# Cross-attention and mixture of experts on one core: the attention slots rewritten as one cyclic schedule

## The chip, the cores and the metric

The kernel runs on one core of one Trainium2 chip. The metric is the device time of one execution, in microseconds (us). A core has five engines that work side by side, each in the order in which its instructions are written: TensorE (PE, with its weight loads shown apart as PEld), VectorE (DVE), ScalarE (ACT), GpSimd (POOL) and SyncE (SP), which here only issues transfers. They wait for one another on semaphores. TensorE writes its results to eight PSUM banks of 512 fp32 columns; DVE and ACT read them from there.

## What is computed

64 sequences `x` of 128 tokens by 128 features attend to 64 contexts of 120 tokens (16 heads of 8 features), and the result goes through a mixture of 8 experts of which each token uses its best two:

```python
x = x + attention(layernorm(x), ctx, ctx)          # softmax over the 120 keys, 16 heads, then Wo
# mixture of experts on h = layernorm(x)
probs = softmax(h @ Wr.T)                          # 8 experts
topv, topi = top_k(probs, 2)
x = x + sum_over_the_two(topv * (gelu(h @ W1[e] + b1[e]) @ W2[e] + b2[e]))
```

## The kernel before, in words

**Chunks and slots.** The 64 sequences go in 32 chunks of two. The attention part is a software pipeline of slots n = -2 to 33, all written out: in slot n the kernel finishes the attention of chunk n and prepares chunk n+1 (its queries) and chunk n+2 (its keys), while chunks n-1 and n-2 get their residual, second layer norm and routing. After the slots come 39 expert tiles of 512 token rows and a last stage that adds the expert results to `xres` and writes the output.

**What one slot does.** The names are those of the tiles in the profile.

- Projections (L1223 to L1225): four groups of six 128x256 matmuls, two for queries and two for keys, each into one bank. ACT takes a part of the bank (`part`, L1056, in `halve`) and DVE subtracts it from the bank into `qs` or `ks` (L711, in `unsplit`).
- SP copies `qs` to `qb` and `ks` to `kb`, four DMAs each (L351, L359). The copies lay the heads out in blocks, so that one matmul serves four heads.
- Scores by query (L1263, `by_query`): eight matmuls of 480 columns; DVE takes the maximum of each over the keys (`mx`, L717, in `best`).
- The maxima are turned on TensorE (L1386), negated and split in an upper and a lower part by DVE (`negm`, L881 and L883), and SP copies them into two rows of `qb` by two DMAs (L384).
- Scores by key (L1273, `by_key`): eight matmuls of 512 columns from `ks` and `qb`, which now hold the maxima too. ACT takes the exponential of each (`pt`, L1065).
- Weighing (L1285, `weigh`): for each exponential, four matmuls with 32-column weights, each at its own column position of the array; a trace shows eight instructions for them. They fill the bank `heads`.
- ACT copies the heads out (`ots`, L1146), TensorE turns them (L1244), DVE divides (`rden` L672, `on` L676), TensorE turns again (L1249), ACT copies (`onT`, L1154), TensorE multiplies by Wo (L1253), DVE adds to `xres` (L686).
- Layer norm: DVE statistics (L827 to L836), a power on GpSimd (`root`, L544), then four small DVE steps (L727 `yy`, L730 `vyy`, L733 `y`, L735 `shift`), ACT applies it.
- Routing: logits (L1394), top two, position of each row in its expert's list, and four scatters by GpSimd (L538). In slots 3 to 18 GpSimd also splits one block of expert weights in upper and lower parts (L602, L604, `wsp`).

**Order.** The order on each engine is the order of the calls in its `slot`. On TensorE each `weigh` is followed by one `by_key`, and `by_query` comes in pairs after them:

```python
for t in range(8):
    weigh(s, t, n)
    if t < 6:
        by_key(s, t + 2, n)
    ...
    if exists(n, 1) and 2 <= t < 6:
        by_query(c, 2 * t - 4, n)
        by_query(c, 2 * t - 3, n)
```

Banks have fixed uses: three (`wide`) for projections and scores by query, two (`scores`) for scores by key, one for `heads`, two (`small`) for everything else. A query goes from its projection through `qs`, the scores by query and the maxima within one slot; the scores by key of that chunk open the next slot.

**The end of attention.** In slot 31 TensorE counts the rows per expert so far (`early`, L1356). On that count SP writes eight 528 KB blocks of empty rows behind the experts' lists (L391, `xd<-zrows`); the last two chunks are scattered over them only afterwards, and the expert tiles read the lists (`rows<-xd`).

## Time and profile before

| | |
|---|---|
| median of 3 runs | 918.71 us (908.99 to 921.09) |
| the profiled execution | 902.89 us, of which the span from first to last instruction is 901.1 us |
| mean granted TensorE clock | 0.932 of full speed |
| attention, first to last slot's scores by key | from 40.5 us to 549 us |
| expert tiles | from 570 us to about 840 us |
| last stage | to 901 us |

Times in rows are microseconds from the span's start. "Busy" is the time in which an engine executes; "idle before" is what stood in front of an instruction on its engine, with what ended that wait.

### The profile page before, as it was taken

What the parts mean: (1) busy time and instruction counts of PE and PEld (TensorE: products, weight loads), DVE (VectorE), ACT (ScalarE), POOL (GpSimd) and SP (SyncE); (2) the same over time, 40 slices, a digit from 0 to 9 for tenths busy, and PEclk for the clock granted to TensorE, in tenths of its full rate; (3) what the DMA queues carried; (4) which work ended last, traced back from release to release, by engine and by line L of the source; (5) the groups of instructions that cost most, each with busy time, mean ns of one, the idle gap of its engine ahead of it and who ended that gap; (6) DMA issues with size and microseconds to landing.
All of it is one profiled execution on the core that took longest, in us unless ns stands there. A gap on an engine that the chain in (4) does not pass through costs nothing.

```text
span 901.1 us, 19693 instructions
## 1 busy us (share of the span) xinstructions
PE 762.4 (85%) x5606; PEld 548.7 (61%) x5606; DVE 670.5 (74%) x2135; ACT 613.6 (68%) x1131; POOL 477.2 (53%) x715
## 2 busy tenths in 40 slices
PE   3699999999999999999999976799889899998700
PEld 3456666566566665666666653588677687777500
DVE  4578889899988898888889873577465666656536
ACT  4677777777777677787777753688585777867500
POOL 4212656656556565554645434447656466675720
PEclk8699999999999999999999995699999899999955
DMA  5333454554545544343433315787666677776059
GB/s 176 97 80 77 116 153 126 135 149 132 154 126 140 150 125 126 106 102 87 99 95 83 88 43 215 234 278 250 212 192 194 197 230 236 228 229 194 18 203 356
DMA packets 117887, 140.33 MB, mean 156 GB/s; under 512 B 20431, under 2 KB 76134, under 8 KB 117799
## 3 DMA queue, kind: packets, MB, share of 16 engines
q1 hardware_dynamic: 105079, 115.72, 45.8%
q0 software_dynamic: 9088, 17.07, 5.5%
q10 hardware_dynamic: 3632, 6.49, 1.9%
q8 instruction: 41, 0.67, 0.3%
q14 instruction: 47, 0.39, 0.1%
HBM read 73.40 MB, written 36.08 MB: 121 GB/s over the span
## 4 chain that ended last, share of the span: by engine, by line
PE 61%; DVE 14%; issue 9%; DMA 5%; SPq 4%; ACT 4%; POOL 2%; another core or an unknown queue 1%; POOLq 0%; DVEq 0%; ACTq 0%
PE bank L1285 8%; PE bank L1273 8%; DVE mx L717 6%; PE bank L1263 5%; PE bank L1442 3%; PE bank L1440 3%; PE bank L1223 3%; PE bank L1441 3%; PE bank L1428 3%; PE bank L1425 3%; PE bank L1426 3%; DMA qb<-yd 3%; PE bank L1244 3%; PE bank L1225 3%; PE bank L1224 3%
## 5 line engine op out<-in xcount | busy, mean ns | idle before, releaser
L642 POOL DMA_INDIRECT yd<-vs,idt x156 | 161.3, 1034 | 105.8 <-DVE vs L991 55.1
L1065 ACT ACTIVATE pt<-bank,mpair 120x512 f32<-120x512 f32 x256 | 171.7, 687 | 48.3 <-PE bank L1273 44.1
L538 POOL DMA_INDIRECT xd<-rows,posi x128 | 130.1, 1016 | 124.4 <-DVE posi L794 77.3
L977 DVE TENSOR_TENSOR qb<-hid,qb 128x512 fp32r<-128x512 f32 x156 | 108.1, 694 | 95.1 <-ACT hid L1180 53.3
L717 DVE TENSOR_REDUCE mx<-bank 128x4 f32<-128x480 f32 x256 | 157.8, 648 | 6.5 <-PE bank L1263 2.7
L1177 ACT ACTIVATE qb<-bank,btile 128x512 fp32r<-128x512 f32 x156 | 109.1, 699 | 66.2 <-PE bank L1442 53.9
L1273 PE MATMUL bank<-qb,ks 128*120 128x512 f32 x256 | 118.7, 484 | 6.9 <-DMA qb<-negm 6.8
L1285 PE MATMUL bank<-pt,vs 120*32 120x128 f32 x2048 | 111.3, 290 | 13.0 <-issue 8.1
L1180 ACT ACTIVATE hid<-bank,btile 128x512 f32<-128x512 f32 x156 | 108.9, 698 | 0.0
L1263 PE MATMUL bank<-kb,qs 128*128 128x480 f32 x256 | 91.9, 411 | 14.9 <-DVE mx L717 14.5
L1285 PEld LDWEIGHTS bank<-pt,vs 120*32 120x32 f32 x2048 | 41.4, 109 | 61.7 <-issue 32.6
L1273 PEld LDWEIGHTS bank<-qb,ks 128*120 128x120 f32 x256 | 44.6, 183 | 48.7 <-issue 39.0
L1263 PEld LDWEIGHTS bank<-kb,qs 128*128 128x128 f32 x256 | 49.0, 191 | 40.8 <-DVE mx L717 36.4
L610 POOL TENSOR_SCALAR rows<-rows 128x256 f32<-128x256 f32 x32 | 13.1, 409 | 84.1 <-ACT rows L1086 84.1
L1056 ACT ACTIVATE part<-bank,liftk,rowselk 128x480 fp32r<-128x480 f32 x64 | 47.8, 748 | 14.3 <-PE bank L1225 14.2
L1056 ACT ACTIVATE part<-bank,liftq,rowselq 128x512 fp32r<-128x512 f32 x64 | 49.1, 771 | 8.3 <-PE bank L1225 7.8
L544 POOL TENSOR_TENSOR y<-ve,minus_half 128x4 f32<-128x4 f32 x36 | 37.5, 1041 | 31.5 <-DVE ve L836 29.1
L711 DVE TENSOR_TENSOR qs<-bank,part 128x512 fp32r<-128x512 f32 x64 | 43.9, 687 | 10.1 <-ACT part L1056 9.5
L1146 ACT ACTIVATE ots<-bank 128x512 f32<-128x512 f32 x64 | 38.3, 598 | 16.5 <-PE bank L1285 14.3
L711 DVE TENSOR_TENSOR ks<-bank,part 128x480 fp32r<-128x480 f32 x64 | 39.5, 646 | 7.0 <-ACT part L1056 6.8
L1223 PE MATMUL bank<-xcTh,wqhi 128*128 128x256 f32 x128 | 42.3, 330 | 2.3 <-DVE xcTl L842 2.3
L1223 PE MATMUL bank<-xcTh,wkhi 128*128 128x256 f32 x128 | 39.6, 309 | 4.9 <-DVE wklo L921 2.7
(200 smaller groups left out, 1964.2 us busy)
## 6 DMA issues: line engine op xcount, KB each, us to landing
kb<-wd SPq DMA_DIRECT2D x40, 512.0 KB
qb<-wd SPq DMA_DIRECT2D x38, 512.0 KB
qb<-qs SPq DMA_DIRECT2D x128, 112.0 KB
kb<-ks SPq DMA_DIRECT2D x128, 105.0 KB
rows<-xd SPq DMA_DIRECT2D x39, 264.0 KB
wd<-wsp SPq DMA_DIRECT2D x16, 512.0 KB
qb<-yd SPq DMA_DIRECT2D x16, 512.0 KB, 6.0
xd<-zrows SPq DMA_DIRECT2D x8, 528.0 KB
```

Of the source, the lines that this page charges most:

```text
L538: g.indirect_dma_start(xd, bass.IndirectOffsetOnAxis(ap=posi[r.phase][:, bk:bk + 1], axis=0), rows[r.phase][:, bk // 2, bk % 2, :], None, ...
L642: g.indirect_dma_start(yd, bass.IndirectOffsetOnAxis(ap=idt[k][:, j:j + 1], axis=0), yrow[p.parity][:, j, :], None, bounds_check=2 * NTOK ...
L717: v.tensor_reduce(mx[:, b, gg, :], wide[m % 3][:, 0:J * KL].rearrange("p (j k) -> p j k", j=J), op=ALU.max, axis=AX.X).then_inc(w_free, 1)
L977: v.tensor_tensor(hhl[:, 1, c, :], hid[:, c % 2, :], hhl[:, 0, c, :], ALU.subtract).then_inc(h_lo, 1)
L1056: a.activation(dst, src, ACT.Identity, bias=lift[int(keys)][:, 0:1], scale=rowsel[int(keys)][:, 0:1]).then_inc(w_part, 1)
L1065: a.activation(pt[t % NP][:].rearrange("p j q -> p (j q)"), scores[t % 2][0:KL, :], ACT.Exp, bias=mpair[s.parity][:, t // G:t // G + 1], s ...
L1177: a.activation(hhl[:, 0, c, :], bank[c][:, :], ACT.Gelu, bias=bias).then_inc(h_hi, 1)
L1180: a.activation(hid[:, c % 2, :], bank[c][:, :], ACT.Gelu, bias=bias).then_inc(h_val, 1)
L1223: t_.matmul(dst, hi, xcTh[f % 2][:, cols], start=True, stop=False)
L1263: t_.matmul(wide[m % 3][:, 0:J * KL].rearrange("p (j k) -> p j k", j=J), qs[c.parity][:, b, g, :], kb[c.parity][:, g, :, b * KL:(b + 1) * ...
L1273: t_.matmul(scores[t % 2][0:KL, :].rearrange("p (j q) -> p j q", j=J), ks[n % 3][:, g, b * KL:(b + 1) * KL], qb[s.parity][:, b, g, :, :], ...
L1285: last = t_.matmul(heads[R * j:R * j + R, g * S:(g + 1) * S], vs[s.parity][:, b, G * g + j, :], pt[t % NP][:, j, :], start=True, stop=True ...
```

## The change

The slots run over n = -5 to 35, and each engine's slot is written as one flat list of small steps, the same in every slot; a step for a chunk that does not exist is left out. What differs:

- **Weighings in fours.** `weigh` of exponentials 0 to 3 stands together, and of 4 to 7. Six buffers `pt` in place of four hold the exponentials meanwhile.
- **Queries a slot ahead.** The projection of queries of chunk n+2 (before: n+1) and of keys of chunk n+3 (before: n+2) is at the end of slot n. The copies of `qs` and `ks` go in turn, across the slot.
- **Five PSUM banks in turn.** Banks 0, 1, 2, 6 and 7 are one ring: 24 uses in a slot, in the order of `UNITS`, each taking the next bank. Before each use TensorE waits until the use five places earlier has been read (`bank_free`).
- **One DMA for both rows of maxima.** `negm` holds the upper and lower part under each other, and one DMA copies 64 rows.
- Two buffers of `mx`; separate semaphores for each kind of work; GpSimd's, DVE's and ACT's steps in another order. Routing of chunk n-3 in place of n-2; the count `early` is taken in slot 32, after chunk 29 as before.

TensorE, one stretch of a slot. Here `bank<-pt,vs` is a weighing, `bank<-qb,ks` a score by key, `bank<-kb,qs` a score by query, `taken` and `before` the routing's counts. Before:

```order
L1285 MATMUL bank<-pt,vs 32x128 x4
L1273 MATMUL bank<-qb,ks 120x512
L1263 MATMUL bank<-kb,qs 128x480 x2
L1347 MATMUL bank<-taken,tri 128x8
L1348 MATMUL bank<-before,ones 128x8
L1347 MATMUL bank<-taken,tri 128x8
L1348 MATMUL bank<-before,ones 128x8
L1350 MATMUL bank<-taken,ones 128x8
L1285 MATMUL bank<-pt,vs 32x128 x4
L1273 MATMUL bank<-qb,ks 120x512
L1263 MATMUL bank<-kb,qs 128x480 x2
L1285 MATMUL bank<-pt,vs 32x128 x4
```

Changed (`onT` is the product with Wo):

```order
L1530 MATMUL bank<-kb,qs 128x480
L1542 MATMUL bank<-qb,ks 120x512
L1530 MATMUL bank<-kb,qs 128x480
L1542 MATMUL bank<-qb,ks 120x512
L1530 MATMUL bank<-kb,qs 128x480
L1557 MATMUL bank<-pt,vs 32x128 x16
L1519 MATMUL bank<-wraw,onT 128x128
L1542 MATMUL bank<-qb,ks 120x512 x2
L1576 MATMUL bank<-ident,rows 128x128 x2
```

Weighings stood alone, eight times in a slot; now 16 matmuls stand together twice in a slot.

SP, the transfers of one slot. Before:

```order
L310 DMA xres<-in_x 128x256
L351 DMA qb<-qs 28x8x128 x4
L359 DMA kb<-ks 28x4x240 x4
L361 DMA kb<-maskd 1x16x240
L314 DMA ctxr<-in_ctx 128x240
L373 DMA wd<-wsp 256x1x512
L379 DMA hid<-in_W 128x512
L384 DMA qb<-negm 1x32x128 x2
```

Changed:

```order
L409 DMA qb<-qs 28x8x128
L364 DMA xres<-in_x 128x256
L409 DMA qb<-qs 28x8x128
L423 DMA kb<-ks 28x4x240
L409 DMA qb<-qs 28x8x128
L423 DMA kb<-ks 28x4x240
L437 DMA kb<-maskd 1x16x240
L409 DMA qb<-qs 28x8x128
L367 DMA ctxr<-in_ctx 128x240
L452 DMA wd<-wsp 256x1x512
L445 DMA qb<-negm 2x32x128
L460 DMA hid<-in_W 128x512
```

The two row copies of the maxima are one, and the copy of the split weights `wsp` now stands right before it.

DVE, from the keys' subtraction on. Before:

```order
L836 TENSOR_SCALAR ve<-mv 128x4
L711 TENSOR_TENSOR ks<-bank,part 128x480 x2
L842 SCALAR_TENSOR_TENSOR xcTl<-bank,xcTh 128x256
L717 TENSOR_REDUCE mx<-bank 128x4
L727 TENSOR_TENSOR yy<-y 128x4
L778 TENSOR_TENSOR place<-bank,region 128x16
L780 TENSOR_TENSOR before<-before,taken 128x8
L717 TENSOR_REDUCE mx<-bank 128x4
L730 SCALAR_TENSOR_TENSOR vyy<-yy,ve 128x4
L717 TENSOR_REDUCE mx<-bank 128x4
```

Changed, from the scores by query to the turned heads of the chunk (`rden`):

```order
L838 TENSOR_REDUCE mx<-bank 128x4
L806 TENSOR_TENSOR xres<-bank,xres 128x128
L1023 TENSOR_TENSOR place<-bank,region 128x16
L1026 TENSOR_TENSOR before<-before,taken 128x8
L877 BN_STATS stats<-xres 128x6 x4
L1035 TENSOR_TENSOR placed<-hot,place 128x16 x2
L787 RECIPROCAL rden<-bank 128x16
L1043 TENSOR_REDUCE posf<-placed 128x4
L1051 CAST posi<-posf 128x4
```

The layer norm's small steps no longer stand between the maxima but at the end of the slot, and the first turned heads are read after the last maximum.

The core of the diff, with TensorE's slot in full but for scores by query and key in its first part:

```diff
-        NP = 4
+        NP = 6
-        negm = [sb(f"negm{k}", [J * G * 2, 2, S], F32R) for k in range(2)]
+        negm = [sb(f"negm{k}", [2 * J * G * 2, S], F32R) for k in range(2)]
...
+        UNITS = (("TO0", -1), ("B0", 1), ("B1", 1), ("B2", 1), ("TX", 2), ("B3", 1), ("B4", 1), ("PO0", -1), ("TO1", -1), ("B5", 1), ("B6", 1), ("B7", 1), ("PO1", -1), ("XR", -2), ("RT", -3), ("M", 1), ("K0", 3), ("TH0", 0), ("LG", -2), ("K1", 3), ("Q0", 2), ("V", 2), ("Q1", 2), ("TH1", 0))
+        pool = [bank[k] for k in (0, 1, 2, 6, 7)]
...
-                    for half in range(2):
-                        row = MHI + half
-                        sp.dma_start(qb[c.parity][row:row + 1].rearrange("a b g j q -> a (b g j) q").bitcast(F32),
-                                     negm[c.parity][:, half, :].bitcast(F32)).then_inc(mrow[c.parity], 16)
+                sp.wait_ge(nm_split, 2 * c + 2)
+                sp.wait_ge(qblk[c % 2], 64 * (c // 2 + 1))
+                sp.dma_start(qb[c % 2][MHI:MHI + 2].rearrange("a b g j q -> a (b g j) q").bitcast(F32),
+                             negm[c % 2][:, :].bitcast(F32)).then_inc(mrow[c % 2], 16)
...
+            def slot(n):
+                score_by_key(n, 0)
+                turn_on(n - 1, 0)
+                score_by_query(n + 1, 0)
+                score_by_key(n, 1)
+                score_by_query(n + 1, 1)
...
+                score_by_query(n + 1, 7)
+                weigh(n, 0)
+                weigh(n, 1)
+                weigh(n, 2)
+                weigh(n, 3)
+                project_out(n - 1, 1)
+                score_by_key(n, 6)
+                score_by_key(n, 7)
+                turn_rows(n - 2)
+                rank(n - 3)
+                turn_maxima(n + 1)
+                project_k(n + 3, 0)
+                turn_heads(n, 0)
+                logits(n - 2)
+                weigh(n, 4)
+                weigh(n, 5)
+                weigh(n, 6)
+                weigh(n, 7)
+                project_k(n + 3, 1)
+                project_q(n + 2, 0)
+                values(n + 2)
+                project_q(n + 2, 1)
+                turn_heads(n, 1)
```

And DVE's slot:

```diff
+            def slot(n):
+                newton_root(n - 1)
+                newton_shift(n - 1)
+                denominators(n - 1, 1)
+                router_sum(n - 3)
+                unsplit_q(n + 1, 1)
+                normalise(n - 1, 1)
+                best(n + 1, 0)
...
+                best(n + 1, 7)
+                residual(n - 1, 1)
+                places(n - 3)
+                statistics(n)
+                places_of(n - 3)
+                denominators(n, 0)
...
+                normalise(n, 0)
+                unsplit_k(n + 3, 0)
+                router_index(n - 2)
+                newton_square(n)
+                newton_times(n)
+                unsplit_k(n + 3, 1)
+                picks(n - 2)
+                unsplit_q(n + 2, 0)
```

## Rows read from the trace of the kernel before

**Rows 1.** The page, busy time, share of the span and instructions of each engine.

```profile
PE 762.4 (85%) x5606; PEld 548.7 (61%) x5606; DVE 670.5 (74%) x2135; ACT 613.6 (68%) x1131; POOL 477.2 (53%) x715
```

**Rows 2.** Windows: length, busy PE, PEld, DVE, ACT, POOL, granted clock, DMA share, GB/s.

```profile
121.41:268.31 146.90, 135.12 (x1225) 91.32 (x1225) 131.88 (x496) 109.82 (x216) 90.14 (x136) 1.00 0.53 140
382.37:476.45 94.08, 89.05 (x817) 61.36 (x818) 83.09 (x331) 72.05 (x144) 48.41 (x79) 1.00 0.38 95
539.11:570.01 30.90, 19.53 (x121) 10.82 (x122) 12.29 (x85) 11.68 (x23) 12.85 (x18) 0.52 0.64 216
```

**Rows 3.** Waits of PE and DVE, 121.41 to 268.31: waiter, waited for, total, times, longest.

```profile
PE bank L1263 <- DVE mx L717: 5.9, 17, 0.6
...
DVE rden L672 <- PE bank L1244: 5.0, 18, 0.4
DVE xcTl L842 <- issue: 3.7, 8, 0.6
```

**Rows 4.** Timeline of PE, full clock: start, length, instruction.

```profile
257.49 0.43 PE L1285 MATMUL bank<-pt,vs 120*32 120x128 f32 x8
257.84 0.50 PE L1273 MATMUL bank<-qb,ks 128*120 128x512 f32 x1
258.18 0.60 PE L1263 MATMUL bank<-kb,qs 128*128 128x480 f32 x2
258.72 0.43 PE L1285 MATMUL bank<-pt,vs 120*32 120x128 f32 x8
```

**Rows 5.** Timeline of PE at the end of attention, the same pair.

```profile
541.67 0.66 PE L1285 MATMUL bank<-pt,vs 120*32 120x128 f32 x8
542.26 0.78 PE L1273 MATMUL bank<-qb,ks 128*120 128x512 f32 x1
```

**Rows 6.** Groups of weight loads, 121.41 to 268.31: count, busy, mean ns, idle before.

```profile
L1273 PEld LDWEIGHTS bank<-qb,ks 128*120 128x120 f32 x73 | 12.5, 180 | 11.1 <-issue 10.7
```

**Rows 7.** Groups of DVE, 121.41 to 268.31.

```profile
L730 DVE SCALAR_TENSOR_TENSOR vyy<-yy,ve 128x4 f32<-128x4 f32 x9 | 6.5, 717 | 0.0
...
L727 DVE TENSOR_TENSOR yy<-y 128x4 f32<-128x4 f32 x9 | 3.6, 401 | 0.0
```

**Rows 8.** The same groups, 382.37 to 476.45.

```profile
L727 DVE TENSOR_TENSOR yy<-y 128x4 f32<-128x4 f32 x6 | 0.9, 152 | 0.0
L730 DVE SCALAR_TENSOR_TENSOR vyy<-yy,ve 128x4 f32<-128x4 f32 x6 | 0.9, 152 | 0.0
```

**Rows 9.** Timeline of SP in one slot: start, time of issue.

```profile
252.26 3.51 SPq L351 DMA_DIRECT2D qb<-qs  x4
256.25 3.36 SPq L359 DMA_DIRECT2D kb<-ks  x4
...
265.14 1.31 SPq L384 DMA_DIRECT2D qb<-negm  x2
```

**Rows 10.** Chain that ended last, in order of time: first scores by key, and of one slot.

```profile
40.51 0.80 PE bank L1273
...
268.31 0.64 PE bank L1273 x2
```

**Rows 11.** Timeline from 538 us: PE, POOL and SP around the end of attention.

```profile
539.11 0.71 PE L1273 MATMUL bank<-qb,ks 128*120 128x512 f32 x2 [0.94 <-DMA qb<-negm]
...
545.58 0.23 PE L1356 MATMUL bank<-before,ones 128*128 128x8 bf16 x1
...
570.01 0.77 PE L1440 MATMUL bank<-kb 128*128 128x512 f32 x1
...
547.47 12.90 SPq L391 DMA_DIRECT2D xd<-zrows  x8
...
578.54 2.98 SPq L421 DMA_DIRECT2D rows<-xd  x2
...
547.39 0.97 POOL L538 DMA_INDIRECT xd<-rows,posi  x1 [0.30 <-issue]
548.67 0.97 POOL L538 DMA_INDIRECT xd<-rows,posi  x1 [0.30 <-issue]
```

More of the change, by code:

```diff
@@ L615, in slot @@
-                if late:
-                    scatter(s + -3, (3,))
-                if exists(n, -2) and n != NCH - 1:
-                    scatter(s + -2, (0,) if exists(n, 1) else (2, 3) if n == NCH else range(4))
-            slots(pool, slot)
+            slots(slot)
             def keep_places(t, n, d):
@@ L1041, in _, with halve_q @@
             a.activation(wq3[0][:], wst[1][:], ACT.Copy).then_inc(wst_hi, 1)
[L1043 to L1045 removed]
+            def halve_q(c, i):
+                if not live(c):
                     return
[L1047 to L1048 removed]
+                if c == 0 and i == 0:
                     act.wait_ge(prep, 1)
[L1050 to L1056 removed]
@@ new lines, in project_q, with project_k @@
+                last.then_inc(q_full, 1)
+            def project_k(c, i):
+                if not live(c):
+                    return
+                if c == 0 and i == 0:
+                    pe.wait_ge(prep, 1)
+                if i == 0:
+                    pe.wait_ge(hl_done, c + 1)
+                turned(pe, bank_free(f"K{i}", c))
+                for gg in range(2):
+                    g = 2 * i + gg
+                    dst = bank_of(f"K{i}", c)[:, gg * KW:(gg + 1) * KW]
+                    hi, lo = (w[:, g].rearrange("p j r -> p (j r)") for w in wk3)
+                    t_.matmul(dst, hi, xcTh[c % 2][:, N2:N2 + KW], start=True, stop=False)
+                    t_.matmul(dst, hi, xcTl[c % 2][:, N2:N2 + KW], start=False, stop=False)
+                    last = t_.matmul(dst, lo, xcTh[c % 2][:, N2:N2 + KW], start=False, stop=True)
+                last.then_inc(k_full, 1)
```

1431 lines of the change are left out of this document (789 added, 642 removed).

## Prediction

> **What bounds the kernel now.** I read the page's busy times first, then the table of windows, then the waits and the timeline of one slot, and last the end of attention. The reader is to see four things.
>
> No engine is full over the span: PE is busy 85%, DVE 74%, ACT 68% [rows 1]. But attention is a different stage from the experts, so it is read alone. From 121.41 to 268.31 us nine slots run, 146.90 us, or 16.32 us a slot; from 382.37 to 476.45 six slots run, 94.08 us, or 15.68 us a slot [rows 2]. The first nine are slots in which GpSimd splits expert weights, the last six are not.
>
> In a slot with the split PE is busy 135.12/9 = 15.01 us and DVE 131.88/9 = 14.65 us; without it PE 89.05/6 = 14.84 us and DVE 83.09/6 = 13.85 us [rows 2]. So both are nearly full, and they wait for each other: PE waits for DVE's maxima in front of the scores by query (5.9 us in nine slots), DVE waits for PE in front of `rden` (5.0 us) and in front of `xcTl` (3.7 us) [rows 3]. ACT needs 109.82/9 = 12.2 us and has room. TensorE runs at full clock in both windows, 1.00 [rows 2].
>
> Not all of PE's busy time is matmul. A weighing starts at 257.49, the score by key behind it at 257.84: 0.35 us [rows 4]. At the end of attention, where the granted clock averages 0.52, the same pair is 0.59 us apart (541.67 to 542.26) [rows 2, 5]. Half the clock doubles only what streams: a + b = 0.35 and 2a + b = 0.59 give a = 0.24 us of streaming and b = 0.11 us that no clock changes, which I take for the emptying of the array before the full-width score. The weight load of the score by key shows the same place: 11.1 us idle before 73 of them, 0.15 us each, put down to issue, that is to nothing the profile can name [rows 6]. And the way into a weighing costs too: two scores by query that a weighing follows take 0.54 us (258.18 to 258.72), against 2 x 0.20 us for 960 columns at 2.4 GHz [rows 4].
>
> **The change, part by part.**
>
> *Weighings in fours.* Eight single weighings become two groups of four. Eight times 0.35 = 2.8 us becomes 2 x (4 x 0.24 + 0.11) = 2.1 us, a gain of 0.7 us of PE per slot. Six of eight entries disappear too: each is worth from 0 to 0.54 - 0.40 = 0.14 us, I take 0.10, 0.6 us; and six scores by key whose weights can now be loaded beforehand, up to 0.15 us each [rows 6]. I take 0.05 for each (their own spacing to the next, 0.34 us at 257.84 to 258.18, is to hold 0.21 us of streaming), 0.3 us. PE's work falls by about 1.6 us, from 15.0 to 13.4 us, with bounds 0.7 and 2.4. PE then is no longer the fuller engine.
>
> *DVE.* Its instructions stay the same ones: none is dropped, none added that counts. So its 13.85 us per slot stands as a floor, and the slot cannot shrink by more than the 1.83 us that DVE now idles (15.68 - 13.85), or 1.67 us with the split. This is what decides the gain. The Trainium skill, page "TensorEngine Tiling (Array Packing)", section "PSUM Bottleneck", speaks against the change in the same sense: packing speeds TensorE, not the reading of its banks. By TensorE's 13.4 us alone the period would be 13.4; by that section it stays at the reader's, and the trace's 13.85 us of DVE agrees.
>
> How much of DVE's idle time is left? `xcTl` and the maxima stop waiting, since scores by query now run from queries that were finished a slot before, and the ring lets PE be up to five banks ahead. What stays is `rden`: DVE reads the turned heads of chunk n behind the last maximum, and between that maximum and them TensorE still has to turn the maxima, do six matmuls of a key projection and turn the heads. Twice 5.0/18 = 0.28 us per slot [rows 3], 0.55 us. Bounds: 0, and the whole 1.83 us. So T = 13.85 + 0.55 = 14.4 us without the split.
>
> *The split.* In slots with it DVE is 14.65 - 13.85 = 0.80 us busier. Two four-column steps hold all of it: `vyy` lasts 717 ns against 152, `yy` 401 against 152, together 0.81 us [rows 7, 8]. Nothing in these instructions differs; they stand beside GpSimd's weight split and end with it. In the new order they stand at the end of the slot, and the split beside maxima, which read PSUM; but `one_hot`, with two SBUF inputs, now stands among these. I take half, 0.4 us, between bounds 0 and 0.8: T = 14.8 us with the split. The Trainium skill, page "SBUF — State Buffer", section "Who interferes with whom", says that a DVE instruction with two SBUF inputs and a GpSimd one that reads SBUF block each other whole, and that a reduction never does. By it the maxima hide the split, and the sum would lose up to 16 x 0.4 = 6.4 us more; `vyy` at 717 ns agrees with the blocking.
>
> *Queries a slot ahead, copies in turn.* SP issues the four query copies at 3.51/4 = 0.88 us each and the keys' at 3.36/4 = 0.84 [rows 9], now interleaved: from the subtraction of the second half of the queries to the last query copy there are four of one, two of the other and three small ones, at most 3.5 + 1.7 + 2.6 = 7.8 us. It has a slot for it. At nothing, hidden beside the eight maxima; if late, see the rivals.
>
> *One DMA for both rows.* From its first issue (265.14) to the next slot's scores by key (268.31) the maxima need 3.2 us [rows 9, 10]. One issue of 1.31/2 = 0.65 us falls away, so 2.5 us; the rest is transfer and notice. Behind the maxima TensorE has key and query projections, a group of weighings and turned heads, over 5 us of work, so neither figure is on the path now: gain 0, bounds 0 and 0.65 us a slot (already inside the bound of DVE's idle time).
>
> *Ends.* From the first scores by key (40.51) to those of slot 31 (539.11) there are 31 periods, 498.6 us [rows 10, 11]. The beginning keeps its parts (zeroing of the block tiles, first copies, maxima), so 0, with bounds of 3 us either way. The last two slots lose their projections: DVE saves four or more subtractions of about 0.6 us each, I take 3 us. The end gets worse. The count `early` is now taken one slot later, behind the output product of chunk 31. It was at 545.58, 6.5 us into slot 31; I put it at about 14 us, because nothing but weighings, turned heads and two products of the last chunk stands before it. Behind it are 12.9 us of issues of empty rows (547.47) and 9.6 us more until the first expert matmul (570.01), which would make 14 + 1 + 12.9 + 9.6 = 37 us against 30.9; but of the 9.6 us part was spent on the last layer norm and routing, which by then is over, so 34 to 35. The last scatters wait for these rows as well: eight of them at 1.28 us (547.39 to 548.67) behind the rows, against a third tile that was loaded at 578.54, 39.4 us into the slot; they would end near 42 [rows 11]. I take +4 us, bounds 0 and +8.
>
> *Sum.* Sixteen of 31 periods have the split: 16 x 14.8 + 15 x 14.4 = 452.8; less 3 for the last two, 449.8, against 498.6: -48.8 us. Plus 4: -44.8. The profiled execution took 902.89 us (span 901.1), so 858.1 us by its own scale. It is 15.8 us under the median of the runs shown, 918.71; the stages that make that spread are not touched, so the predicted median is 918.71 - 44.8 = 873.9 us, rounded to 874.
>
> **The rivals.**
>
> *A, more gain.* DVE never waits and the split costs nothing: 31 x 13.85 - 3 = 426.4, -72.2, and +2 at the end: -70, 849 us. For it: `rden` is the only wait that I could name, and DVE's small steps are spread so that none follows its own input. Against: ten or more hand-overs per slot must all be in time.
>
> *B, little change.* The ring of five binds PE, ACT and DVE more tightly than three plus two plus two banks did: every one of the 24 uses waits for its reader, in order, and one late reader stops all engines in turn. If this leaves DVE 1.65 us idle per slot, T = 15.5 in all: 31 x 15.5 = 480.5, -18, +4: -14, 905 us. For it: the order is fixed beforehand, and a slot of the old order with three banks lost 0.65 us before the scores by query alone (5.9/9). Against: PE has 1 us of room now.
>
> *C, slower.* The queue of SP in front of the maxima. The scores by key of chunk n+1 wait for: subtraction of the queries 0.7, up to 7.8 us of issues, landing L of the last copy, for which SP waits, and 2.5 us for the maxima. These 11.0 + L us, and some 13 us from those scores to the end of the query projection two slots on, must fit in two periods: 2T = 24 + L. At L = 2.5, as the maxima's copy shows, this is 13.3 us and hidden. From L = 8.6 us on it exceeds 16.3 us and the kernel is slower. The place where it could happen is the split weights' copy, which SP now issues right before the maxima and for which it waits on GpSimd. At T = 17.0: 31 x 17.0 = 527, +28, +4: 951 us. For it: the DMA share is already 0.53 in these slots [rows 2]. Against: nothing in the trace shows a landing of 8 us.
>
> *D, the change does what it says but the end eats it.* The end would have to lose 45 us; its bound is 8. Not given a chance of its own.
>
> **How the numbers follow.** Forecast 0.64, A 0.17, B 0.13, C 0.06. The forecast's own spread, T from 13.9 to 15.3 around the sum, is 852 to 898. The range 849 to 906 takes A's and B's values in and leaves most of C and the far sides of A and B out. Faster or slower by over 2% (18 us), about what a measurement of this kernel can tell from no change: faster holds nearly all of the forecast and A, 0.82; within 2% a little of the forecast and most of B, 0.12; slower C, 0.06.
>
> **What would show it.** Right: periods of 14.2 to 15.0 us from one slot's first score by key to the next; DVE busy over 93% of the attention windows, PE below it; four weighings in a row at about 0.24 us each; `vyy` near 152 ns; the rows of empty blocks issued some 15 us after slot 31's first score by key. Wrong: DVE idle of over 1.2 us per slot with waits on PE or ACT spread over many lines (B); the scores by key waiting for `negm` or SP busy up to the maxima's copy (C); weighings in a group still 0.35 us apart, by which PE would stay at 14.3 us and the period with it.

## The result, and the profile after

The changed kernel takes 865.8 us (median of four runs, 856.7 to 874.9), the kernel before beside it 919.9 us: a ratio of 0.950, with a 95% interval of 0.938 to 0.963. (The ratio is taken over the fast executions of both alone and is therefore not the quotient of the medians, which is 0.941.) The prediction was 874 us, with a range of 849 to 906. The profiled execution took 867.83 us, its span is 866.1 us.

The page, where [rows 1] had 85% for PE and 74% for DVE:

```profile
PE 708.0 (82%) x5606; PEld 564.3 (65%) x5606; DVE 646.7 (75%) x2135; ACT 612.0 (71%) x1131; POOL 474.3 (55%) x715
```

Windows of the changed kernel, with the columns of [rows 2]: fourteen slots, of which thirteen have the weight split; eleven without it; slot 31 up to the first expert matmul; the expert tiles; and the thirteen slots with the split alone.

```profile
94.11:306.17 212.06, 187.58 (x1915) 149.45 (x1909) 199.72 (x773) 169.36 (x337) 136.34 (x207) 0.98 0.54 147
306.17:453.25 147.08, 144.23 (x1506) 115.26 (x1498) 137.90 (x608) 132.47 (x265) 88.28 (x143) 1.00 0.45 109
481.92:519.57 37.65, 16.10 (x136) 11.66 (x137) 15.16 (x114) 12.70 (x28) 21.32 (x31) 0.64 0.53 184
519.57:810.33 290.76, 263.03 (x1221) 212.40 (x1222) 176.94 (x277) 207.89 (x350) 167.49 (x225) 0.94 0.65 203
94.11:292.78 198.67, 174.35 (x1777) 138.95 (x1771) 187.22 (x717) 157.91 (x313) 128.28 (x194) 0.98 0.55 150
```

A slot without the split takes 147.08/11 = 13.37 us (15.68 before). PE is busy in 144.23/147.08 = 98% of it, 13.11 us, and DVE 137.90/11 = 12.54 us. So PE is the full engine, not DVE, and DVE's 12.54 us lie under the 13.85 us that the prediction called its floor. A slot with the split takes 198.67/13 = 15.28 us (16.32 before), and there both engines have gaps.

Where the time went, by the two profiles: the first scores by key start at 43.38 in place of 40.51 (+2.9); from them to those of slot 31 there are 438.5 us in place of 498.6 (-60.1); from there to the first expert matmul 37.65 in place of 30.9 (+6.75); from it to the end 346.5 in place of 331.1 (+15.4, expert tiles and last stage, whose code the change does not touch). The sum is -35.0, and 901.1 - 866.1 = 35.0.

A group of four weighings, timeline of PE, where [rows 4] had single ones 0.35 us long:

```profile
386.00 1.08 PE L1557 MATMUL bank<-pt,vs 120*32 120x128 f32 x32
387.01 0.38 PE L1481 MATMUL bank<-xcTh,wkhi 128*128 128x256 f32 x1
387.23 0.29 PE L1482 MATMUL bank<-xcTl,wkhi 128*128 128x256 f32 x1
387.35 0.28 PE L1483 MATMUL bank<-xcTh,wklo 128*128 128x256 f32 x1
```

Four weighings take 387.01 - 386.00 = 1.01 us; the prediction had 4 x 0.24 + 0.11 = 1.07. The matmul behind the first full-width one starts 0.22 us after it, the next ones at distances of 0.12.

What engines wait for from 94.11 to 306.17 (waiter, waited for, total, times, longest):

```profile
PE bank L1519 <- DVE xres L806: 10.5, 6, 1.9
PEld bank L1542 <- DMA qb<-negm: 8.5, 14, 1.0
...
PEld bank L1598 <- DVE taken L1001: 6.6, 7, 1.0
...
PE bank L1542 <- DMA qb<-negm: 5.2, 12, 0.8
PE bank L1598 <- DVE taken L1001: 4.9, 7, 0.7
```

And one such slot in the timelines of DVE, POOL and PE:

```profile
209.29 0.70 DVE L973 TENSOR_TENSOR hot<-pick,eidx 128x16 bf16<-128x16 f32 x2
209.91 0.64 DVE L838 TENSOR_REDUCE mx<-bank 128x4 f32<-128x480 f32 x1
210.48 1.89 DVE L993 TENSOR_TENSOR taken<-hot 128x16 bf16<-128x16 bf16 x1
212.30 0.15 DVE L964 RECIPROCAL tinv<-tsum 128x2 f32<-128x2 f32 x1
212.37 0.26 DVE L806 TENSOR_TENSOR xres<-bank,xres 128x128 f32<-128x128 f32 x1
...
210.05 0.99 POOL L646 DMA_INDIRECT xd<-rows,posi  x1 [0.17 <-issue]
211.06 1.28 POOL L692 TENSOR_TENSOR wsp<-hid,wsp 128x512 fp32r<-128x512 f32 x1
...
212.78 0.69 PE L1519 MATMUL bank<-wraw,onT 128*128 128x128 f32 x2 [1.79 <-DVE xres L806]
213.12 1.20 PE L1542 MATMUL bank<-qb,ks 128*120 128x512 f32 x2
```

`taken`, 16 columns of bf16, lasts 1.89 us and ends with GpSimd's lower weight split (L692, to 212.34). Behind it stands `xres`, which empties the bank that PE wants for the next output product, and PE is idle 1.79 us. After the pause its next matmuls run at the lower clock: two scores by key last 1.20 us, against 0.71 at full clock, and the granted clock is 0.54 in the window from the pause on (it is 1.00 from 198 to 210 us):

```profile
212.78:216.50 3.72, 3.72 (x21) 3.34 (x22) 2.51 (x12) 1.62 (x4) 0.00 (x0) 0.54 0.60 198
```

Six of the thirteen slots have such a pause of TensorE, 1.48 to 1.89 us long, behind a `taken` (in one of them a `hot`) of 1.9 to 2.0 us. The clock falls behind two of these pauses, and those slots take 17.0 us; behind the other four it stays at 1.00, and they take 15.3 to 15.6. So the pause costs 0.7 to 1.0 us against the slots next to it, and the lower clock, where it comes, 1.4 more. In the remaining seven the second `taken` (L1001) is held 1.63 us, only the routing's count on TensorE (L1598) waits for it, and the slot takes 14.6 to 14.8 us. How many slots are of which kind changes from execution to execution: in two more profiles of the same kernel (below) only one slot has the long pause, and the mean with the split is 14.7 us.

DVE's small steps in the slots without the split (306.17 to 453.25; in those of the kernel before, 382.37 to 476.45, `ve` lasted 519 ns and `hot` 311 ns):

```profile
L973 DVE TENSOR_TENSOR hot<-pick,eidx 128x16 bf16<-128x16 f32 x22 | 2.7, 166 | 0.0
...
L904 DVE SCALAR_TENSOR_TENSOR vyy<-yy,ve 128x4 f32<-128x4 f32 x11 | 1.8, 163 | 0.4
L892 DVE TENSOR_SCALAR ve<-mv 128x4 f32<-128x4 f32 x11 | 1.8, 163 | 0.0
```

### The profile page after: what moved, and what is told of

It reads as the page before. It is cut to its first block, busy times and chain, and to the rows that moved or that the text cites. A ratio compares the mean times of both kernels' runs of the same rounds, so it can differ in the third digit from the quotient of the medians.

```text
span 866.1 us, 20430 instructions
## 1 busy us (share of the span) xinstructions
PE 708.0 (82%) x5606; PEld 564.3 (65%) x5606; DVE 646.7 (75%) x2135; ACT 612.0 (71%) x1131; POOL 474.3 (55%) x715
## 4 chain that ended last, share of the span: by engine, by line
issue 29%; PE 28%; POOL 26%; DMA 5%; ACT 3%; DVE 3%; SPq 2%; another core or an unknown queue 2%; POOLq 0%; ACTq 0%; DVEq 0%
POOL xd L646 10%; PE bank L1706 4%; PE bank L1704 4%; PE bank L1705 3%; PE bank L1689 3%; PE bank L1692 3%; PE bank L1690 3%; POOL xres L625 3%; DMA qb<-yd 3%; POOL wsp L692 2%; POOL y L653 2%; POOL xcTl L669 2%; PE bank L1620 2%; POOL yd L757 1%
## 5 line engine op out<-in xcount | busy, mean ns | idle before, releaser
L757 POOL DMA_INDIRECT yd<-vs,idt x156 | 158.6, 1017 | 120.5 <-DVE vs L1209 73.8
L1292 ACT ACTIVATE pt<-bank,mpair 120x512 f32<-120x512 f32 x256 | 165.1, 686 | 9.9 <-PE bank L1542 6.3
L1542 PE MATMUL bank<-qb,ks 128*120 128x512 f32 x256 | 110.9, 455 | 15.4 <-DMA qb<-negm 12.7
L1530 PE MATMUL bank<-kb,qs 128*128 128x480 f32 x256 | 99.2, 423 | 2.6 <-DMA kb<-maskd 1.0
L1557 PE MATMUL bank<-pt,vs 120*32 120x128 f32 x2048 | 70.0, 278 | 0.0
L1279 ACT ACTIVATE part<-bank,liftk,rowselk 128x480 fp32r<-128x480 f32 x64 | 48.3, 757 | 18.3 <-PE bank L1483 18.1
L1557 PEld LDWEIGHTS bank<-pt,vs 120*32 120x32 f32 x2048 | 52.6, 110 | 8.7 <-issue 7.3
L1704 PE MATMUL bank<-kb 128*128 128x512 f32 x80 | 34.4, 430 | 16.9 <-DVE kb L1121 15.6
L1481 PE MATMUL bank<-xcTh,wkhi 128*128 128x256 f32 x128 | 43.8, 342 | 3.9 <-DVE wklo L1089 2.7
L827 DVE TENSOR_TENSOR ks<-bank,part 128x480 fp32r<-128x480 f32 x64 | 41.7, 652 | 3.3 <-ACT part L1279 3.3
L1504 PE MATMUL bank<-ident,ots 128*128 128x128 f32 x256 | 39.1, 276 | 1.9 <-ACT ots L1301 1.0
```

What stands on the lines that cost most here:

```text
L757: g.indirect_dma_start(yd, bass.IndirectOffsetOnAxis(ap=idt[k][:, j:j + 1], axis=0), yrow[p.parity][:, j, :], None, bounds_check=2 * NTOK ...
L1292: a.activation(pt[m % NP][:].rearrange("p j q -> p (j q)"), scores[t % 2][0:KL, :], ACT.Exp, bias=mpair[c % 2][:, t // G:t // G + 1], scal ...
L1530: t_.matmul(bank_of(f"B{u}", c)[:, 0:J * KL].rearrange("p (j k) -> p j k", j=J), qs[c % 2][:, b, g, :], kb[c % 2][:, g, :, b * KL:(b + 1) ...
L1542: t_.matmul(scores[t % 2][0:KL, :].rearrange("p (j q) -> p j q", j=J), ks[c % 3][:, g, b * KL:(b + 1) * KL], qb[c % 2][:, b, g, :, :], sta ...
L1557: last = t_.matmul(heads[R * j:R * j + R, g * S:(g + 1) * S], vs[c % 2][:, b, G * g + j, :], pt[(8 * c + t) % NP][:, j, :], start=True, st ...
L1704: t_.matmul(bank[c][:, :], w[:, 0, 0, cs], xh, start=True, stop=False)
```

## Experiments

The runs were made in groups, each beside the kernel before, and the groups lie on two levels: the kernel before has a median of 873.5 to 874.0 us in three of them and of 919.9 in two, the result above included. I call these the 874 level and the 920 level; the recorded expectations speak of two chips. That the level belongs to a chip is not shown: the record numbers the chips 9, 1 and 10 at the 874 level, and 1 again at the 920 level. The same kernel's slots without the split differ by less than 0.1 us between the levels (13.30 and 13.36 us), its expert tiles by over 40 us. So each total is compared with the kernel before of its own group, and slots are read in the profiles, as the distance between two `negm`.

**1. The split beside the maxima** (874 level)

```diff
                 second_rows(n - 3)
+                upper_weights(n + 2)
+                lower_weights(n + 2)
                 scatter(n - 4, 0)
...
-                upper_weights(n + 2)
                 scatter(n - 4, 2)
-                lower_weights(n + 2)
```

Expected: 

> The changed kernel, with GpSimd's two steps of the weight split moved in its list from behind the third scatter to right behind `rows` (second_rows), so that they run beside the first maxima, which read PSUM, and no longer beside the routing's small steps `hot` and `taken`. Theory: the slots with the split take 15.15 us instead of 13.36 because one small DVE step on SBUF operands is held for the length of the lower split (`taken` 1.63 to 1.89 us instead of 0.15) and TensorE then loses its clock. So periods of 13.4 to 13.8 us in the slots with the split, `taken` and `hot` near 0.15 each, total 20 to 28 us under the changed kernel. Rival: the 512 KB copies of the split weights that SP issues in front of the maxima cost the time; then the periods stay at 14.6 us or more. The periods without the split stay at 13.36 us by both.

Measured: 801.4 us, ratio 0.918 (0.916 to 0.920). Thirteen slots with the split take 13.3 to 14.4 us, and `taken` is 0.14 to 0.19 us in all of them. It was run again beside the changed kernel, at the 874 level.

Expected: 

> The kernel with the split beside the maxima once more, beside the changed kernel on one chip. On the first chip its slots with the split took 13.3 to 14.4 us; the two kernels built on it took 14.6 to 15.0 us on another chip, on which `ots` and `xres` waited up to 2 us in each such slot. If that wait belongs to the other order of SP's copies, this one takes 13.3 to 14.4 us on any chip and is 2 to 3% under the changed kernel; if it belongs to the chip, 14.6 to 15.0 us there, and no gain.

Expected of the changed kernel: 

> The changed kernel on the same chip as the run beside it: periods of 14.6 us with the split, single ones of 15.6 to 17.0, and 13.26 to 13.36 without it. The expert stage takes 248 us if this is the chip of the first experiments, 280 to 294 if it is the other.

Measured: 802.8 us against 820.1 us; ratios to the kernel before 0.9205 (0.917 to 0.924) and 0.9415 (0.937 to 0.946). Windows of the second run, thirteen slots with the split and eleven without it:

```profile
95.61:271.26 175.65, 169.05 (x1776) 135.88 (x1771) 167.02 (x717) 156.69 (x313) 127.81 (x194) 1.00 0.62 167
284.54:430.93 146.39, 143.26 (x1505) 114.73 (x1501) 138.16 (x608) 132.09 (x265) 88.08 (x143) 1.00 0.46 110
```

175.65/13 = 13.51 us with the split, PE busy 96%, and 146.39/11 = 13.31 without it; the changed kernel beside it takes 14.70 us with the split. 16 x 1.2 = 19 us explain the 17.3 us between the two. The copy of the split weights still stood in front of the maxima, so that copy did not cause the long slots. What is left is mostly `hot`: its two steps last up to 1.1 us where they stand beside GpSimd's `xres` (L625) and `xcTl`, and they end with these:

```profile
130.99 1.07 DVE L973 TENSOR_TENSOR hot<-pick,eidx 128x16 bf16<-128x16 f32 x2
...
130.45 0.89 POOL L625 TENSOR_TENSOR xres<-xres,bob 128x128 f32<-128x128 f32 x2
131.28 0.74 POOL L669 TENSOR_TENSOR xcTl<-ctxr,xcTh 128x256 fp32r<-128x256 f32 x1
```

**2. Single weighings in the new order** (874 level)

```diff
+                weigh(n, 0)
                 score_by_query(n + 1, 7)
-                weigh(n, 0)
                 weigh(n, 1)
+                project_out(n - 1, 1)
                 weigh(n, 2)
+                score_by_key(n, 6)
                 weigh(n, 3)
-                project_out(n - 1, 1)
-                score_by_key(n, 6)
                 score_by_key(n, 7)
```

(and weighings 4 to 7 in the same way between logits and the two halves of the key projection)

Expected: 

> The changed kernel, with each weighing again between full-width matmuls (scores by query, output product, scores by key, logits, halves of the key projection), all else in place. Theory of the prediction: six more ways in and out of the column-tiled form cost TensorE 6 x (0.11 + 0.10 + 0.05) = 1.6 us a slot, and as TensorE is busy 98% without the split, the period there goes from 13.36 to 14.9 us. Rival: the gain came from the order and the ring, and single weighings cost little: 13.4 to 13.8 us.

Measured: 904.5 us, ratio 1.035 (1.033 to 1.037). Eleven slots without the split, then the twelve slots with it from 118.30 on, and four rows of PE:

```profile
353.55:526.50 172.95, 165.69 (x1498) 112.97 (x1497) 142.88 (x608) 130.50 (x265) 88.47 (x143) 1.00 0.38 93
118.30:337.84 219.54, 196.76 (x1634) 134.37 (x1633) 175.03 (x663) 143.24 (x289) 119.31 (x180) 0.91 0.45 124
```

```profile
401.48 0.28 PE L1484 MATMUL bank<-xcTh,wklo 128*128 128x256 f32 x1
401.69 0.43 PE L1559 MATMUL bank<-pt,vs 120*32 120x128 f32 x8
402.05 0.38 PE L1482 MATMUL bank<-xcTh,wkhi 128*128 128x256 f32 x1
402.27 0.28 PE L1483 MATMUL bank<-xcTl,wkhi 128*128 128x256 f32 x1
```

The slot without the split takes 15.72 us, 2.41 more than with fours at the same level (13.31), and PE is busy 165.69/11 = 15.06 us, 2.04 more (143.26/11 = 13.02). The rows show one single weighing: 0.09 us to enter it (401.48 to 401.69, less the 0.12 of a matmul), 0.36 in place of 0.25 for itself, 0.10 to leave it (0.22 in place of 0.12 at 402.05). That is 0.30 us for each that goes, 1.8 us for six; the prediction had 0.26 and 1.6. Of the other 0.6 us, 0.4 is idle time of PE; why was not shown. The slots with the split lose more, and most of the total: they take 219.54/12 = 18.3 us, where the changed kernel takes 14.7. In ten of the twelve `hot` is held 1.9 us, and TensorE's granted clock is 0.91 on average. So the 84 us between this total and the changed kernel's 820.1 are not the price of the column-tiled form alone; that price is read from the 2.41 us.

**3. Weighings in fours in the old order** (874 level)

```diff
-        NP = 4
+        NP = 6
...
-                        weigh(s, t, n)
+                        for w in {3: range(4), 7: range(4, 8)}.get(t, ()):
+                            weigh(s, w, n)
                         if t < 6:
                             by_key(s, t + 2, n)
```

Expected: 

> The kernel before, with the weighings 0 to 3 and 4 to 7 together and six buffers of exponentials, nothing else changed. Theory: TensorE's busy time falls by 1.6 us a slot to about 13.3, but the slot only shortens by what DVE and the chain of query, maxima and scores by key let it: from 15.68 to between 14.3 and 15.0 us without the split. Rival one: fours are the whole gain, 13.4 us. Rival two: the slot is bound by its chain of waits, and the period stays within 0.3 us of 15.68.

Measured: 877.7 us against 873.6, ratio 1.004 (1.003 to 1.006). Eight slots without the split, and their waits:

```profile
361.79:490.35 128.56, 111.58 (x1090) 85.33 (x1089) 108.79 (x440) 95.35 (x193) 64.62 (x104) 1.00 0.38 92
```

```profile
PEld bank L1263 <- DVE mx L717: 13.2, 16, 1.2
...
ACT pt L1065 <- PE bank L1273: 6.5, 8, 1.5
...
PE bank L1263 <- DVE mx L717: 6.3, 8, 0.8
DVE negm L881 <- PE bank L1387: 5.7, 8, 0.7
DVE mx L717 <- PE bank L1263: 4.8, 8, 0.6
```

(The sixth buffer takes the place of a tile of zeros, and one GpSimd step is written without that tile.) PE's busy time falls to 111.58/8 = 13.95 us, but the slot takes 16.07 us on average (seven of 15.95 to 15.98 and one of 16.80), not less than before. PE and DVE wait for each other at the three banks of the scores by query, in both directions. The theory of this run, 14.3 to 15.0 us, is refuted. Rival two is the nearest, though its bound of 0.3 us over 15.68 is just passed: with the old order fours alone buy nothing.

**4. A ring of four banks** (920 level, with the changed kernel once more as its base)

```diff
-        pool = [bank[k] for k in (0, 1, 2, 6, 7)]
+        pool = [bank[k] for k in (0, 1, 2, 6)]
```

Expected: 

> The changed kernel with a ring of four PSUM banks in place of five. Rival B of the prediction: the ring, used in a fixed order, is what binds the engines. Then one bank less costs 0.5 to 1.5 us a slot (13.8 to 14.8 without the split). Theory: PE is busy 98% with five, so the ring has room to spare by what DVE is behind; four cost little, up to 0.3 us a slot.

Expected of the base: 

> The changed kernel itself once more, as the base for the runs beside it on this chip. The first experiments ran on a chip on which the slots without the split take 13.26 us and whose TensorE runs the expert stage at 0.99 of its clock (0.94 in the profile of the changed kernel). Expected: if the 15 us that the unchanged expert stage was longer in the profile of the changed kernel came from that run's clock, then on a chip with a full clock this kernel takes 270 to 275 us from the first expert tile to the last, like the kernel before there; if they come from the change, 10 us or more longer than the kernels built on the kernel before.

Measured: 936.1 us, ratio 1.017 (1.009 to 1.025); the base 865.9 us, 0.939 (0.927 to 0.950). Nine slots without the split and their waits:

```profile
374.29:514.77 140.48, 123.00 (x1233) 93.48 (x1227) 116.25 (x497) 109.26 (x217) 72.04 (x117) 0.99 0.38 93
```

```profile
PE bank L1519 <- DVE mx L838: 8.1, 8, 1.0
...
DVE xres L806 <- PE bank L1519: 6.9, 9, 0.8
ACT pt L1292 <- PE bank L1542: 6.3, 9, 0.8
DVE xcTl L860 <- ACT xcTh L1330: 5.6, 9, 0.6
```

One bank less costs 15.61 - 13.36 = 2.25 us a slot, nearly all of the 2.3 that the change had won there: my theory of this run (up to 0.3 us) was wrong by far, and rival B's 0.5 to 1.5 us was too small as well. (The total exceeds the kernel before's because the slots with the split take 16.6 to 18.4 us here.) The waits are those of rival B, on many lines and in turn: PE waits for a maximum to free its bank, DVE for the product that PE could not start.

**5. Two DMAs for the maxima in the changed kernel, one in the kernel before** (both at the 874 level)

```diff
-                sp.dma_start(qb[c % 2][MHI:MHI + 2]...
-                             negm[c % 2][:, :].bitcast(F32)).then_inc(mrow[c % 2], 16)
+                for half in range(2):
+                    row = MHI + half
+                    sp.dma_start(qb[c % 2][row:row + 1]...
```

Expected: 

> The changed kernel, with the two rows of maxima copied by two DMAs again. The prediction priced the one DMA at nothing: then 13.36 us a slot without the split stays, within 0.1. Rival, after the trace of the changed kernel, where the first scores by key wait for this copy: one more issue of about 0.65 us in front of them, of which TensorE has few other things to do: 13.8 to 14.0 us, some 15 us in all.

Expected of the other way round: 

> The kernel before with one DMA for both rows of maxima, nothing else. Theory of the prediction: hidden, 0 in all. Rival: in the old order the scores by key that open a slot stand right behind this copy, and one issue of 0.65 us falls away in each: up to 0.65 us a slot, 20 us in all.

Measured: the changed kernel with two takes 816.3 us, ratio 0.935 (0.931 to 0.939), 13.26 us a slot without the split. That is the same slot as with one, and the totals' intervals (0.931 to 0.939, 0.937 to 0.946), from two groups of runs, overlap, so nothing is shown against one DMA there. The kernel before with one takes 880.5 us, ratio 1.008 (1.005 to 1.011): slower, which neither the theory nor the rival of that run had. The waits for this copy, each from 300 to 440 us; first the changed kernel at the 874 level, then the same with two DMAs:

```profile
PEld bank L1542 <- DMA qb<-negm: 3.9, 10, 0.6
PE bank L1542 <- DMA qb<-negm: 1.7, 6, 0.4
```

```profile
PEld bank L1545 <- DMA qb<-negm: 1.1, 4, 0.5
PE bank L1545 <- DMA qb<-negm: 0.2, 1, 0.2
```

One copy of 32 KB is waited for longer than two of 16 KB, although one issue fewer stands in front of it. In the old order, where nearly no slot waited, the same edit brought 3.6 us of such waits in nine slots. The semaphore events of the traces agree: the last one of this copy comes 3.2 us after its issue began, and 2.8 us after the first of the two issues began (medians of 32); in the old order 3.3 against 2.55. So the one DMA lands later, although one issue of 0.6 us is gone. Why it does was not tested.

**6. The maxima's copy ahead of the weights' copy, and `xcTl` ahead of the scatter** (920 level; both with experiment 1's edit in place)

```diff
-                save_weights(n + 3)
                 copy_maxima(n + 1)
+                save_weights(n + 3)
```

Expected: 

> The kernel with the split beside the maxima (the first experiment), and in SP's list the copy of the maxima ahead of the copy of the split weights. In that experiment the scores by key still waited for the maxima 8.2 us in 13 slots with the split, and single periods were 13.9 to 14.4 us. Theory: the 512 KB copy in front of the maxima is what made these (rival C, small): the longer periods fall to 13.3 and the total by 2 to 5 us. Rival: they come from `hot`, held by GpSimd's `xcTl` (1.0 us in place of 0.25 in two of them); then little changes, under 1 us.

Expected with `lower_ctx` before `scatter(n - 4, 0)` in addition: 

> The former kernel, and GpSimd's lower part of the contexts (`xcTl`) ahead of its first scatter, so that `hot` of VectorE no longer stands beside it. Theory: `hot` is 0.25 us for two in all slots and no period with the split is over 13.4: 1 to 4 us less than the former. Rival: the hold moves to another small step of VectorE, and nothing is gained.

Measured: 858.9 and 859.6 us, ratios 0.934 (0.926 to 0.942) and 0.937 (0.929 to 0.946), not told apart from the changed kernel's 0.939 (0.927 to 0.950) in that group. Both fail: with the split beside the maxima these slots should take 13.5 us, and all but the first take 14.6 to 15.0. The wait for the maxima is about half (3.4 us of weight loads' waits between 123 and 284 us, 6.4 in the base), but another came, in each of these slots, at the same place:

```profile
164.35 0.60 ACT L1301 ACTIVATE ots<-bank 128x512 f32<-128x512 f32 x1 [2.12 <-remote]
```

`ots` starts 2.1 us late, though the weighings in front of it end near 161.7, and `xres` on DVE 1.6 us late at 164.39. The profile names no instruction that released them ("remote"), but both wait for TensorE's own semaphores, and the semaphore events of the trace have these late: TensorE's matmuls that the profile ends (by its model) between 161.77 and 163.85 are signalled together, between 164.32 and 164.65. The changed kernel at this level has the same in small: from 109 to 433 us, the latest signal of each full slot comes 0.8 to 1.2 us after the modelled end, with the split and without it, and at the 874 level 0.2 us or less. Experiment 1, which was run at the 874 level alone, has up to 0.6. So the late signals belong at least in part to the level. What holds them, and whether the weights' copy, now in flight at the head of the slot, or the split's new place makes them 2 us late here, stays open, and with it whether experiment 1's gain is to be had at the 920 level. In the second run `hot` also got longer, 0.77 to 1.09 us: it was now held by another GpSimd step, `xres` (L625). The rival of that run, that nothing is gained, holds, though it expected another step of VectorE to be held.

**7. Split beside the maxima, and two DMAs** (874 level)

Expected: 

> Both edits that did no harm together: the split beside the maxima (first experiment) and two DMAs for the maxima. In the first experiment TensorE still waited for the one DMA of maxima 8.2 us in the 13 slots with the split (weight loads), and some of these slots took 13.9 to 14.4 us. If the one DMA of 32 KB lands later than two of 16 KB, these waits shrink and the kernel takes 2 to 6 us less than with the split beside the maxima alone (ratio to the kernel before 0.912 to 0.918 where that one has 0.918 to 0.9205). Rival: the longer slots come from `hot`, held beside GpSimd's `xcTl`; then no difference that can be measured. Without the split 13.26 us a slot by both, or 13.36 on the chip on which the expert stage is slow.

Measured: 800.8 us, ratio 0.9175 (0.916 to 0.919), against 0.918 and 0.9205 of experiment 1: no difference that can be measured. Slots with the split are 13.3 us, or 13.9 where `hot` is at 0.8 to 1.1 us; the rival's cause. At this level both versions are faster than the kernel before and the changed kernel.

## Why the prediction came out right, step by step

**Its total.** 874 was forecast, 865.8 measured, and the change of the medians is -54 us for -44.8. By the profiles the attention won 60.1 us where 48.8 were forecast, the end lost 6.75 for 4, the beginning 2.9 for 0. That would make -50.4. The profiled executions differ by only 35.0, because the tiles and the last stage took 15.4 us longer, nearly all in the tiles (290.8 us for 275.2). At the 874 level the change does not lengthen them: the changed kernel took 247.7 us for the tiles, kernels built on the kernel before 250.2 and 250.5. At the 920 level it is not shown: the changed kernel and those built on it took 280 to 298 us in five profiles, the kernel before 275.2 in its only one. But that one execution, of 902.9 us, was 17 us under the median of its kernel, and I take the 15.4 us to be this, an inference. The granted clock in the tiles was 0.94 in the profile of the changed kernel and 0.99 in the same kernel's at the 874 level, where PE is busy throughout:

```profile
510.55:758.22 247.67, 247.15 (x1221) 204.26 (x1222) 180.10 (x277) 214.81 (x350) 168.00 (x224) 0.99 0.75 238
```

What makes the levels differ there was not looked for.

**"Weighings in fours: PE's work falls by about 1.6 us": right in kind, a little small.** Measured 15.06 - 13.02 = 2.04 us (experiment 2); from [rows 2] to the changed kernel's window it is 14.84 - 13.11 = 1.73 us. The way in and out of a single weighing is 0.30 us, not 0.26.

**"PE then is no longer the fuller engine", "13.85 us per slot stands as a floor": wrong.** This is the step that failed. DVE's busy time fell from 13.85 to 12.54 us a slot without one of its 55 instructions dropped. DVE is busy 93.8% of the window, as forecast ("over 93%"), but PE is above it and not below, and the slot of 13.37 us lies outside the 14.2 to 15.0 that were named as the sign of being right. A busy time was taken for work, but it holds two things that belong to the order. Some steps were held beside GpSimd: `ve` 519 ns where 163 do, `hot` 311 where 166 do, 0.36 and twice 0.15 us a slot; the durations of the 55 steps add up to 17.0 us before and 16.3 after. And steps that follow without a pause overlap (L964 starts at 212.30 and lasts 0.15, the next starts at 212.37), so that each pause between them adds to the busy time: the trace has 14 pauses a slot of any length before and 8 after, and 3.1 and 3.8 us of overlap; that is the other 0.7 us. The forecast T of 14.4 us was thus 1.0 us too long; by PE's own 13.4 us, which the text works out and sets aside, the slot without the split comes out right. (The 13.4 starts from the 15.0 us of slots with the split; from the 14.84 without it the same sum gives 13.2.) The sentence of the Trainium skill that was weighed, page "TensorEngine Tiling (Array Packing)", section "PSUM Bottleneck", that packing speeds TensorE and not the reading of its banks, did not set the period here: it would give 13.85 us by [rows 2], and the trace shows 13.37 with PE at 98%.

**"`rden` stays, 0.55 us": replaced.** Without the split `rden` isn't among the waits. In its place DVE waits 5.2 us in ten of these waits for the output product, in front of `xres`; its idle time is 0.83 us a slot in all, where 1.83 was before. With the split `rden` stays, 4.5 us in thirteen waits. The prediction also put the 3.7 us in front of `xcTl` down to PE; [rows 3] names no releaser for them.

**"I take half, 0.4 us" for the split: too small, and for another reason.** The split cost 15.28 - 13.37 = 1.9 us a slot in this profile, and 1.4 in the two others of the kernel. `vyy` is at 163 ns beside the split as without it, near the 152 forecast, but `taken` and `hot` took its place, up to 2.0 us each. The hold can cost more than its length, 3.6 us in the two slots of 17.0, since DVE's `xres` behind it frees a bank of the ring, TensorE stands still until then, and its clock can fall. Experiment 1 shows it: moved beside the maxima, the same split costs 13.51 - 13.31 = 0.2 us. The Trainium skill, page "SBUF — State Buffer", section "Who interferes with whom", has both halves of this, the blocking of two SBUF inputs and the freedom of reductions. The prediction used both, but of the steps with two SBUF inputs among the maxima it named only `hot`, and left out `taken`. By that rule the trace agrees: `taken` 1.89 us beside the split, 0.15 us otherwise. The rows add that it had begun at 210.48, before the step with which it ended began (211.06).

The two errors have opposite signs. The sixteen slots with the split took 239.6 us (the first three, in which the routing is not yet full, 13.0 to 14.2 each), 2.8 more than the 16 x 14.8 forecast; the rest took 14.1 less than 15 x 14.4 - 3. Together that is the 11.3 us by which the attention won more than forecast, and the loss at both ends took back 5.6 of them. That the total came within 8 us is thus partly luck: the limiting engine of most slots was the wrong one.

**"One DMA: gain 0": right**, by experiment 5. But its reason, that the maxima's copy is off the path, no longer holds once the slot is at 13.4 us: 3.9 us of waits in ten slots. And its term, 2.5 us for the copy with one issue less, was wrong: the one DMA lands 3.2 us after its issue began. In the old order the edit costs 0.8%.

**Rival B, "the ring binds": not at five banks, fully at four.** **Rival C, the queue of SP: refuted** for the weights' copy by experiment 1. **Rival A** ("DVE never waits") was the nearest for the slots without the split, where DVE still idles 0.83 us, and even these fell below its 13.85. Two of the recorded sums are not consistent with the forecast's: B and C leave out its 3 us for the last two slots, and so does the upper end of the spread, which would be 895 and not 898. And the 2.6 us put down for three small issues of SP is more than three of its other small issues take, 0.56 to 0.62 us each. None of this moves the forecast.

**The end.** The count stood 14.7 us into slot 31 (14 forecast), the eight issues took 12.82 us. The 9.6 us behind them were forecast to shrink by 2 to 3 us, as the last layer norm would be over. They are still 8.7 us: SP issues the first rows at 513.44, they are there at 517.07, and turning them and the steps up to the first expert matmul take until 519.57. No layer norm is among these:

```profile
498.05 12.82 SPq L484 DMA_DIRECT2D xd<-zrows  x8
...
517.07 1.09 PE L1620 MATMUL bank<-ident,rows 128*128 128x128 f32 x4 [8.93 <-DMA rows<-xd]
...
519.57 0.79 PE L1704 MATMUL bank<-kb 128*128 128x512 f32 x1 [1.41 <-DVE kb L1121]
```

**What made the gain.** Slots without the split:

| | single weighings | in fours |
|---|---|---|
| old order | 15.68 us (kernel before) | 16.07 us (experiment 3) |
| new order, ring of five | 15.72 us (experiment 2) | 13.26 to 13.37 us |
| new order, ring of four | not run | 15.61 us (experiment 4) |

Neither part gains anything alone. Fours take work from an engine that the old order lets wait (PE busy 13.95 of 16.07 us); the new order takes waits from an engine that single weighings keep full (15.06 of 15.72). What in the new order does it, the queries a slot ahead or the ring, was not separated beyond the fourth bank.

## What to carry to other kernels

The busy time of an engine that has pauses is no floor: take from it what small steps last longer than their fastest copies, and read it again in a stretch without pauses. Two edits that each gain nothing can gain all together, when each takes away one of two limits of the same height; so test the pair before dropping either. And when work moves on GpSimd, look at what small step of VectorE with two inputs in SBUF will stand beside it, and at which bank is freed behind that step.

## What the runs showed of the hardware

- A VectorE step of 16 bf16 columns took 1.89 us in place of 0.15, up to the end of a GpSimd step of 1.28 us that had not begun when it started; before it GpSimd issued a scatter.
- A pause of 1.79 us of TensorE in a full slot was followed by 3.7 us at a granted clock of 0.54 (two scores by key 1.20 us in place of 0.71), and the slot was 17.0 us long where most with the split take 14.6. This happened behind two of six such pauses; behind four others, of 1.48 to 1.89 us, the clock stayed at 1.00 and the slots took 15.3 to 15.6.
- One column-tiled group between full-width matmuls costs 0.09 us on the way in and 0.10 on the way out, in the rows of experiment 2.
- One DMA of 64 rows of 512 bytes landed 3.2 us after its issue began, two of 32 rows 2.8 us after the first issue began, and the one was waited for more (3.9 against 1.1 us of weight loads' waits in 140 us).
- The same kernel differs by 46 us between two groups of runs (865.9 and 820.1), nearly all in the expert tiles (294.3 and 247.7 us), while its attention slots without the split differ by less than 0.1 us each.
- In two kernels at the 920 level TensorE's semaphore signals came together, up to 2.5 us after the ends that the profile gives the matmuls; in the changed kernel 0.8 to 1.2 us at that level and 0.2 or less at the other.
